# The order of VectorE's and ScalarE's work in the node stage of a graph network: statistics, scales and features ahead of the MLP's first addition

## The chip, the cores and the metric

One core of one Trainium2 chip. The metric is the device time of one execution in microseconds (us), lower is better, median of 3 runs. All data are float32.

## The reference

A graph of 12,500 nodes with 256 features and 200,000 edges with 96 features, sorted by destination. Two layers, each added to its input; cut to what matters:

```python
h = relu(layernorm(x))
# layer 0: an MLP on the node and what its incoming edges give
out1 = segment_sum(edge_attr, dst); cnt = segment_sum(1, dst)
out2 = where(cnt > 0, segment_max(edge_attr, dst), 0)
out3 = out1 / maximum(cnt, 1)
f = concatenate([h, out1, out2, out3, u[0]], axis=1)       # 256 + 3*96 + 64
x1 = x + (relu(f @ W1 + b1) @ W2 + b2) + h                 # W1: 608 x 1024, W2: 1024 x 256
# layer 1: two graph attention layers over the edges
h1 = relu(layernorm(x1))
g = gat(h1, W=g1, heads=4)                                 # first step of it: h1 @ g1
out = x1 + gat(elu(g), W=g2, heads=1)
```

## The kernel before

The kernel is a sequence of stages with a barrier of all engines behind each: `edge_chains` (sums and maxima of the edges' features, and already the part h @ W1 of the MLP, which goes to memory as `pre`), `node_mlp` (the node stage, the one that the change touches), `attention` and `close_first`, and again `attention` and `close_last`.

**The node stage** works on 49 tiles of 256 nodes. Every engine runs a function `step` for n = -1 to 49, the middle ones in a hardware loop, two steps per turn. Nothing but the order written in each engine's `step`, and semaphores between them, sets when what is done. In step n the stage has three tiles in hand:

- `nxt`, tile n+1: its input x is normalised (VectorE `statistics(nxt, 0)`, ScalarE `roots`, VectorE `inverse(nxt, 0)`, ScalarE `normal(nxt, 0)`, which writes h), and its edge features are scaled into `feat` (`features`, L1318 to L1322) for TensorE to transpose.
- `at`, tile n: the MLP. TensorE makes the first layer in four products of two chunks of 128 hidden columns each, 8 matmul records per product (L1138). VectorE adds `pre` to each product (`add_first(at, 0)` to `add_first(at, 3)`, L1332), ScalarE takes the Relu (`hidden`, L1206), TensorE makes the second layer (L1194).
- `prev`, tile n-1: VectorE adds the second layer to the residual (`result`, L1279; the result is x1), then its statistics (bn_stats L1261, bn_aggr L1265, variance L1267), ScalarE the root (L1210), VectorE `inverse(prev, 1)` (L1271, L1273), ScalarE the normalised rows h1 (L1215), TensorE transposes h1 (L1160), VectorE copies the transposed rows (L1367), and TensorE projects them with `wg` (L1185).

TensorE's order in a step: products 0 to 2 of `at`; the transposes of `prev`'s h1, ahead of which it waits for them; product 3; the transposes of `nxt`'s features (L1170, L1177); then twice a projection for `prev` (L1185) and a half of the second layer for `at` (L1194).

VectorE's order behind what the diff shows: the copy L1367 stands between `add_first(at, 2)` and `add_first(at, 3)`; then the copies of the transposed features, the two projections' outputs with `joined_edges` between them (L1302, L1308: edge rows for the tile after next), the rows x1 for memory (L1290), and `residual` (L1337, L1339), which reads h of `nxt`.

SP loads x and `pre` for the step after next and stores x1 and the projected rows. GpSimd, released by `joined_edges`, issues per step four gathers of single edges (L1095), two gathers of edge sums (L1102) and, from the tile with number 6 on, two scatters of scores to memory (L1110).

Of the kernel before, what the change touches and what calls it, by code (L numbers as in the profile page):

```python
# [954 lines left out]
def node_mlp(nc, s, io, dr, keep):  # L955
# [9 lines left out]
    KK = HC // 2  # L965
# [3 lines left out]
    with stage(nc, "node_mlp") as (c, sem):  # L969
# [74 lines left out]
        def all_steps(eng, step, first=-1):  # L1044
            steps(eng, first, LOOP, LOOP_END, NS + 1, step)
# [155 lines left out]
        @block.scalar  # L1201
        def _(a):
            def hidden(at, kk):
                a.wait_ge(m1_added, at.n * KK + (kk + 3))
                pair = hid[:, at.par, 2 * kk:2 * kk + 2, :]
                a.activation(pair, pair, ACT.Relu).then_inc(hid_ready, 1)  # L1206

            def roots(at, w):
                a.wait_ge(var_ready[w], at.n + 1)
                a.activation(root[:, w, :], var[:, w, :], ACT.Sqrt).then_inc(root_ready[w], 1)  # L1210

            def normal(at, w, src, dst, done):
                a.wait_ge(nb_ready[w], at.n + 1)
                for t in range(2):
                    a.activation(dst[:, t, :], src[:, t, :], ACT.Relu, bias=nb[:, w, t:t + 1],  # L1215
                                 scale=rstd[:, w, t:t + 1]).then_inc(done, 1)

            def step(at, n):
                nxt, prev = at.plus(1), at.plus(-1)
                mlp = n is None or 0 <= n < NS  # L1220
                if n is None or n >= 1:
                    roots(prev, 1)
                if mlp:
                    hidden(at, 0)
                if n is None or n + 1 < NS:
                    roots(nxt, 0)
                if n is None or n >= 1:
                    normal(prev, 1, x1[:, prev.par, :, :], h1[:, :, :], h1_ready)
                if mlp:
                    hidden(at, 1)  # L1230
                    hidden(at, 2)
                if n is None or n + 1 < NS:
                    normal(nxt, 0, x[:, nxt.par, :, :], hrow[:, nxt.par, :, :], h_ready)
                if mlp:
                    hidden(at, 3)

            a.dma_start(wg[:, :, 0:XF], io["g1_w"].rearrange("(k p) n -> p k n", p=P)).then_inc(wg_in, 16)
            for m, name in enumerate(("g1_src", "g1_dst")):
                a.dma_start(att[:, m, :], io[name].rearrange("h d -> (h d)").unsqueeze(0)
                            .to_broadcast([P, XF])).then_inc(wg_in, 16)  # L1240
            a.dma_start(g2b[:, :], io["g2_b"].unsqueeze(0).to_broadcast([P, XF])).then_inc(g2b_in, 16)
            a.dma_start(g1b[:, 0:XF], io["g1_b"].unsqueeze(0).to_broadcast([P, XF])).then_inc(g1b_in, 16)
            a.dma_start(wg2[:, :, 0:XF], io["g2_w"].rearrange("(k p) n -> p k n", p=P)).then_inc(late_in, 16)
            for m, name in enumerate(("g2_src", "g2_dst")):
                a.dma_start(att2[:, m, :], io[name].rearrange("h d -> (h d)").unsqueeze(0)
                            .to_broadcast([P, XF])).then_inc(late_in, 16)
            all_steps(a, step)

        @block.vector
        def _(v):  # L1250
# [25 lines left out]
            def result(at, n):  # L1276

                v.wait_ge(m2_ready, at.n + 1)
                v.tensor_tensor(x1[:, at.par, :, :], res[:, at.par, :, :],  # L1279
                                pM2[:, :].rearrange("p (t f) -> p t f", t=2), ALU.add).then_inc(x1_ready, 1)  # L1280
                v.wait_ge(x1_ready, at.n + 2)
                statistics(at, 1, x1[:, at.par, :, :])
# [44 lines left out]
            def add_first(at, kk):  # L1327

                if kk == 0:
                    v.wait_ge(pre_in[at.par], at.half * 16 + 16)  # L1330
                v.wait_ge(m1_ready, at.n * KK + (kk + 1))
                v.tensor_tensor(hid[:, at.par, 2 * kk:2 * kk + 2, :].rearrange("p k n -> p (k n)"), pM1[kk][:, :],  # L1332
                                pre[:, at.par, 2 * kk:2 * kk + 2, :].rearrange("p k n -> p (k n)"), ALU.add).then_inc(m1_added, 1)
# [8 lines left out]
            def step(at, n):  # L1342
                nxt, prev = at.plus(1), at.plus(-1)
                back = n is None or n >= 1
                front = n is None or n + 1 < NS
                mlp = n is None or 0 <= n < NS
                if back:
                    result(prev, None if n is None else n - 1)
                if mlp:
                    add_first(at, 0)  # L1350
                if front:
                    v.wait_ge(x_in[nxt.par], nxt.half * 16 + 16)
                    statistics(nxt, 0, x[:, nxt.par, :, :])
                if back:
                    inverse(prev, 1)
                if mlp:
                    add_first(at, 1)
                if front:
                    inverse(nxt, 0)
                    if n is not None and n <= 1:  # L1360
                        joined_edges(nxt, n + 1)
                    features(nxt)
                if mlp:
                    add_first(at, 2)
                if back:
                    v.wait_ge(gt_ready, prev.n + 1)
                    v.tensor_copy(h1T[:, :, :].rearrange("p i n -> p (i n)"), pG[:, :]).then_inc(gt_copied, 1)  # L1367
                if mlp:
                    add_first(at, 3)
                if front:  # L1370
                    v.wait_ge(t_ready, nxt.n + 1)
                    v.tensor_copy(fT[:, nxt.par, 0:2, :].rearrange("p i n -> p (i n)"), pF0[:, :])
                    v.wait_ge(rest_ready, nxt.n + 1)
                    v.tensor_copy(fT[:, nxt.par, 2, :], pF1[:, 0:N2]).then_inc(t_copied, 1)
                if back:
                    for t in range(2):
                        v.wait_ge(go_ready, prev.n * 2 + (t + 1))
                        if t == 0 and (n is None or n >= 3):
                            v.wait_ge(g_out[prev.par], prev.half * 16)
                        v.tensor_copy(keep["ald"][:, bass.ds(prev.n * 2 + t, 1), :].rearrange("p o h -> p (o h)"),  # L1380
                                      pGo[:, XF + H:WG]).then_inc(ald_ready, 1)
                        v.tensor_copy(keep["als"][:, bass.ds(prev.n * 2 + t, 1), :].rearrange("p o h -> p (o h)"),
                                      pGo[:, XF:XF + H])
                        if n is not None and t == 0 and prev.n == 0:
                            v.wait_ge(g1b_in, 16)
                            v.wait_ge(g1b_filled, 1)
                        v.tensor_tensor(grow[:, prev.par, t, :], pGo[:, 0:WG], g1b[:, :], ALU.add).then_inc(go_copied, 1)
                        if t == 0 and (n is None or n + 2 < NS):
                            joined_edges(at.plus(2), None if n is None else n + 2)
                if back:  # L1390
                    biased(prev, None if n is None else n - 1)
                if front:
                    if n == -1:
                        v.wait_ge(b2_in, 16)
                    residual(nxt)
                if n == 0:
                    v.wait_ge(wg_in, 16 * 3)
                    project_attention(v, chain, wg, att, tmp, H)
                    v.sem_inc(projected, 1)
                    v.memset(g1b[:, XF:WG], 0.0).then_inc(g1b_filled, 1)  # L1400
                    v.wait_ge(edges_in, 32)
                    v.tensor_scalar(keep["dst0"][:, :], dst0[:, :], s.NP - 1, None, ALU.min)
                if n == 16:
                    v.wait_ge(late_in, 16 * 3)
                    project_attention(v, chain, wg2, att2, tmp, 1)
                    v.sem_inc(wg2_ready, 1)
# [4 lines left out]
            v.sem_inc(go_copied, 1)  # L1411
            v.sem_inc(m1_added, 2)
            all_steps(v, step)


# [366 lines left out]
```

## Time and profile before

| | |
|---|---|
| median of 3 runs | 6822.59 us (6811.17 to 6826.57) |
| the profiled execution's own time | 6822.27 us |
| span of that execution | 6820.3 us |
| busy share of the span: TensorE, VectorE, ScalarE, GpSimd | 23%, 68%, 46%, 58% |
| node stage, first to last `result` (L1279) | 702.8 to 1793.9 us |

The profile is of one execution. An engine counts as busy while one of its instructions runs; waits and DMA issues don't count. In the rows further down, PE is TensorE, PEld its weight loads, DVE VectorE, ACT ScalarE, POOL GpSimd; L1279 is line 1279 of the kernel. PEclk is the share of TensorE's full clock of 2.4 GHz that was granted; its two levels are 1.0 and 0.5 (1.2 GHz). Matmul ends are modelled. The releaser of a wait is inferred from semaphore events; "remote" and "issue" mean that no instruction was found that ended it.

### The profile page before, as it was taken

The page shows a single profiled execution, that of the slowest core. Times are in us where ns is not written, and L with a number is a line of the kernel's source. Part 1 is how long each engine was busy: PE and PEld are TensorE (multiplying, and loading weights), DVE is VectorE, ACT ScalarE, POOL GpSimd, SP SyncE. Part 2 cuts the span into 40 slices and gives each one's busy share as a digit, 9 for nine tenths or more (in the row PEclk, how much of TensorE's full clock was granted, in tenths as well). Part 3 has the DMA queues.
Part 4 walks back from the last instruction along what each step waited for, and adds up shares of the span by engine and source line. Part 5 has one row for each costly group of instructions (what it writes and reads, how often), then busy time and mean ns, then how long its engine had stood idle before and what let it go on. Part 6 is the DMA issues. An engine that isn't in the chain of part 4 may idle for free. (4 is left out here: it accounts for less than half of the span.)

```text
span 6820.3 us, 34527 instructions
## 1 busy us (share of the span) xinstructions
PE 1577.0 (23%) x7221; PEld 1277.1 (19%) x7221; DVE 4656.6 (68%) x8059; ACT 3168.9 (46%) x2937; POOL 3988.8 (58%) x3935
## 2 busy tenths in 40 slices
PE   6675888888500000000000004500000000000000
PEld 4554676766400000000000003400000000000000
DVE  8997656656567777777776674466766766766665
ACT  7984222222145555555554552345555555555540
POOL 1330333333466666667666646577777777777756
PEclk9998999999755555555555557755555555555555
DMA  9998332332355555555555544456555555555548
GB/s 339 372 381 312 103 106 93 100 97 93 101 190 188 187 187 190 193 192 198 197 185 184 189 175 128 108 178 205 183 184 201 184 184 196 188 184 189 189 164 302
DMA packets 358516, 1281.83 MB, mean 188 GB/s; under 512 B 83184, under 2 KB 175408, under 8 KB 328272
## 3 DMA queue, kind: packets, MB, share of 16 engines
q1 hardware_dynamic: 167984, 756.10, 29.9%
q0 software_dynamic: 180320, 471.38, 24.0%
q10 hardware_dynamic: 10048, 52.70, 1.9%
q14 instruction: 127, 1.04, 0.0%
q8 instruction: 37, 0.61, 0.0%
HBM read 676.46 MB, written 603.41 MB: 188 GB/s over the span
## 5 line engine op out<-in xcount | busy, mean ns | idle before, releaser
L162 POOL DMA_INDIRECT rows<-table_d,k_src x3128 | 3123.2, 998 | 1256.3 <-issue 1142.5
L217 ACT ACTIVATE rows<-totals 128x1472 f32<-128x1472 f32 x544 | 2088.9, 3863 | 1408.9 <-DVE totals L308 1042.9
L308 DVE TENSOR_TENSOR_SCAN totals<-mask,turned 128x1536 f32<-128x1536 f32 x544 | 1806.4, 3341 | 71.1 <-DMA g1b<-in_g_b 60.7
L180 PE MATMUL pB<-diag,k_ones 128*128 128x512 f32 (+1 forms) x4 | 2.9, 822 | 4405.9 <-DVE diag L327 2222.0
L299 DVE TENSOR_TENSOR turned<-rows,pT 128x1472 f32<-128x1472 f32 x544 | 916.1, 1684 | 0.0
L180 PEld LDWEIGHTS pB<-diag,k_ones 128*128 128x128 f32 x4 | 1.0, 312 | 4406.6 <-DVE diag L327 2222.3
L1095 POOL DMA_INDIRECT lone_ea<-in_ea,k_gather x196 | 202.1, 1031 | 640.4 <-DVE mid_feat L1308 565.6
L265 DVE TENSOR_TENSOR z<-rows,ad 128x92 f32<-128x92 f32 (+1 forms) x136 | 29.0, 214 | 643.0 <-DMA rows<-table_d,k_src 596.0
L720 PE MATMUL pH<-hT_pre,w1h 128*128 128x256 f32 x1568 | 410.6, 419 | 135.6 <-ACT hT_pre L598 109.3
L1138 PE MATMUL pM<-fT,w1e 128*128 128x256 f32 x1568 | 405.0, 416 | 1.5 <-issue 1.5
L1194 PE MATMUL pM<-w,hid 128*128 128x256 f32 x1568 | 360.1, 383 | 1.8 <-issue 1.3
L720 PEld LDWEIGHTS pH<-hT_pre,w1h 128*128 128x128 f32 x1568 | 320.6, 211 | 210.5 <-ACT hT_pre L598 125.0
L209 ACT ACTIVATE pT<-zm 128x92 f32<-128x92 f32 (+1 forms) x136 | 29.5, 217 | 666.3 <-issue 410.9
L1138 PEld LDWEIGHTS pM<-fT,w1e 128*128 128x128 f32 x1568 | 317.6, 208 | 64.6 <-issue 18.9
L664 POOL DMA_INDIRECT dst_rows<-in_dst,full_i x98 | 149.6, 1527 | 306.9 <-DVE full_i L779 279.0
L1332 DVE TENSOR_TENSOR hid<-pM,pre_in 128x512 f32<-128x512 f32 x196 | 134.9, 689 | 258.8 <-PE pM L1138 211.5
L1194 PEld LDWEIGHTS pM<-w,hid 128*128 128x128 f32 x1568 | 296.9, 191 | 52.7 <-ACT hid L1206 10.0
L1210 ACT ACTIVATE root<-var 128x2 f32<-128x2 f32 x98 | 19.9, 203 | 582.6 <-DVE var L1267 323.6
L1206 ACT ACTIVATE hid<-hid 128x512 f32<-128x512 f32 x196 | 122.7, 626 | 338.2 <-DVE hid L1332 337.1
L1439 POOL DMA_INDIRECT acc_c<-sums_d,k_gather x196 | 211.0, 1077 | 76.0 <-issue 60.7
L910 DVE SCALAR_TENSOR_TENSOR run<-run,joins,duo 128x96 f32<-128x96 f32 x783 | 243.5, 311 | 2.4 <-DMA rows_d<-run 1.5
L910 DVE SCALAR_TENSOR_TENSOR run<-run,parts_off,duo 128x96 f32<-128x96 f32 x783 | 243.4, 311 | 0.0
(248 smaller groups left out, 3808.7 us busy)
## 6 DMA issues: line engine op xcount, KB each, us to landing
sums_d<-rows SPq DMA_DIRECT2D x68, 3036.0 KB
sums_d<-rows SPq DMA_DIRECT2D x68, 2967.0 KB
ea<-in_ea SPq DMA_DIRECT2D x98, 768.0 KB
rows_d<-run SPq DMA_DIRECT2D x97, 768.0 KB
pre_d<-pre ACTq DMA_DIRECT2D x49, 1024.0 KB
pre_in<-pre_d SPq DMA_DIRECT2D x49, 1024.0 KB
rows<-table_d,k_src POOLq DMA_INDIRECT x3128
hrow_c<-table_d SPq DMA_DIRECT2D x98, 256.0 KB
```

Of the source, the lines that this page charges most:

```text
L162: p.indirect_dma_start(out=rows[:, g.slot, k, :], out_offset=None, in_=table, in_offset=bass.IndirectOffsetOnAxis(ap=keep["src"][:, e:e + ...
L217: a.activation(rows[:, g.slot, :, q * PD:(q + 1) * PD], totals[:, q, :, 1:].rearrange("p d k -> p k d"), ACT.Copy).then_inc(rowed, 1)
L299: return link.mark(v.tensor_tensor(into[:, :, 1:].rearrange("p d k -> p k d"), rows[:, g.slot, :, q * PD:(q + 1) * PD], weights[:, :, h:h ...
L308: v.tensor_tensor_scan(totals[:, q, :, :].rearrange("p d k -> p (d k)"), mask[:, g.n % 2, :, :].rearrange("p d k -> p (d k)"), turned[q % ...
L664: g.indirect_dma_start(out=rows[:, b % 2, q, :], out_offset=None, in_=tiles_of("dst"), in_offset=bass.IndirectOffsetOnAxis(ap=full_i[:, b ...
L720: mm = pe.matmul(pH[k % 4][:, 0:N2], w1h[:, i, k * P:(k + 1) * P], hT[:, n % 2, i, :], start=(i == 0), stop=(i == 1))
L910: v.scalar_tensor_tensor(out=run[:, g % BUFS, k, m, :], in0=before, scalar=by[:, e:e + 1], in1=duo[:, g % 2, m, k, :], op0=op0, op1=op1).t ...
L1095: g.indirect_dma_start(out=lone_ea[:, n % 2, t, i, :], out_offset=None, in_=io["ea"], in_offset=bass.IndirectOffsetOnAxis(ap=keep["gather" ...
L1138: mm = pe.matmul(pM1[kk][:, h * N2:(h + 1) * N2], w1e[:, i, cols], fT[:, at.par, i, :], start=False, stop=(i == 1), skip_group_check=True)
L1194: mm = pe.matmul(pM2[:, t * XF:(t + 1) * XF], hid[:, at.par, k, t * P:(t + 1) * P], w2[:, k, :], start=(k == 0), stop=(k == HC - 1), skip_ ...
L1332: v.tensor_tensor(hid[:, at.par, 2 * kk:2 * kk + 2, :].rearrange("p k n -> p (k n)"), pM1[kk][:, :], pre[:, at.par, 2 * kk:2 * kk + 2, :]. ...
L1439: g.indirect_dma_start(out=self.acc[:, n // PER % 2, j % self.CH, :], out_offset=None, in_=self.rows, in_offset=bass.IndirectOffsetOnAxis( ...
```

## The change

Only the order of calls in two `step` functions of the node stage differs. On VectorE `add_first(at, 0)` and `add_first(at, 1)` go behind `features(nxt)`. On ScalarE all four `hidden` go behind `normal(prev, 1, ...)` and ahead of `normal(nxt, 0, ...)`.

```diff
@@ ScalarE, step @@
                 if n is None or n >= 1:
                     roots(prev, 1)
-                if mlp:
-                    hidden(at, 0)
                 if n is None or n + 1 < NS:
                     roots(nxt, 0)
                 if n is None or n >= 1:
                     normal(prev, 1, x1[:, prev.par, :, :], h1[:, :, :], h1_ready)
                 if mlp:
-                    hidden(at, 1)
-                    hidden(at, 2)
+                    for kk in range(KK):
+                        hidden(at, kk)
                 if n is None or n + 1 < NS:
                     normal(nxt, 0, x[:, nxt.par, :, :], hrow[:, nxt.par, :, :], h_ready)
-                if mlp:
-                    hidden(at, 3)
@@ VectorE, step @@
                 if back:
                     result(prev, None if n is None else n - 1)
-                if mlp:
-                    add_first(at, 0)
                 if front:
                     v.wait_ge(x_in[nxt.par], nxt.half * 16 + 16)
                     statistics(nxt, 0, x[:, nxt.par, :, :])
                 if back:
                     inverse(prev, 1)
-                if mlp:
-                    add_first(at, 1)
                 if front:
                     inverse(nxt, 0)
                     if n is not None and n <= 1:
                         joined_edges(nxt, n + 1)
                     features(nxt)
                 if mlp:
+                    add_first(at, 0)
+                    add_first(at, 1)
                     add_first(at, 2)
```

## Rows read from the trace of the kernel before

**Rows 1.** Timeline of VectorE: start us, us, instruction, idle before and its releaser.

```profile
745.97 0.69 DVE L1279 TENSOR_TENSOR x_rows<-res,pM 128x512 f32<-128x512 f32 x1 [0.96 <-issue]
...
1738.86 0.69 DVE L1279 TENSOR_TENSOR x_rows<-res,pM 128x512 f32<-128x512 f32 x1 [0.81 <-PE pM L1194]
...
1757.26 0.69 DVE L1279 TENSOR_TENSOR x_rows<-res,pM 128x512 f32<-128x512 f32 x1 [0.81 <-PE pM L1194]
```

**Rows 2.** Waits of 746 to 1739 us: total us, times, longest.

```profile
DVE hid L1332 <- PE pM L1138: 200.3, 75, 4.6
...
PE pG_ L1160 <- ACT h_rows L1215: 153.8, 43, 6.4
```

**Rows 3.** Timeline of one step, 1226.07 to 1248.04, engine by engine.

```profile
1226.07 0.69 DVE L1279 TENSOR_TENSOR x_rows<-res,pM 128x512 f32<-128x512 f32 x1 [0.82 <-PE pM L1194]
...
1232.64 0.69 DVE L1332 TENSOR_TENSOR hid<-pM,pre_in 128x512 f32<-128x512 f32 x1 [4.49 <-PE pM L1138]
1233.25 0.74 DVE L1261 BATCH_NORM_STATS2 bn_st<-x_rows 128x6 f32<-128x256 f32 x2
...
1235.79 0.32 DVE L1318 TENSOR_SCALAR feat<-mid_feat,has 128x192 f32<-128x192 f32 x1
...
1236.97 0.69 DVE L1332 TENSOR_TENSOR hid<-pM,pre_in 128x512 f32<-128x512 f32 x1
1237.57 0.68 DVE L1367 COPY h1T<-pG_ 128x512 f32<-128x512 f32 x1
1238.52 0.69 DVE L1332 TENSOR_TENSOR hid<-pM,pre_in 128x512 f32<-128x512 f32 x1 [0.27 <-PE pM L1138]
...
1248.04 0.69 DVE L1279 TENSOR_TENSOR x_rows<-res,pM 128x512 f32<-128x512 f32 x1 [0.81 <-PE pM L1194]
...
1234.89 1.09 ACT L1215 ACTIVATE h_rows<-x_rows,nb,rstd 128x256 f32<-128x256 f32 x2
...
1227.03 5.45 PE L1138 MATMUL pM<-fT,w1e 128*128 128x256 f32 x24
1236.13 0.63 PE L1160 MATMUL pG_<-k_ident,h_rows 128*128 128x128 f32 x4 [3.65 <-ACT h_rows L1215]
...
1239.93 3.72 PE L1194 MATMUL pM<-w,hid 128*128 128x256 f32 x16
...
1230.18 0.98 POOL L1110 DMA_INDIRECT first_d<-k_ald,k_first  x1 [0.30 <-issue]
```

**Rows 4.** Timeline of two other steps: GpSimd's last of four scatters, VectorE's additions.

```profile
1718.78 0.97 POOL L1110 DMA_INDIRECT first_d<-k_ald,k_first  x1 [0.31 <-issue]
...
1721.41 0.69 DVE L1332 TENSOR_TENSOR hid<-pM,pre_in 128x512 f32<-128x512 f32 x1 [7.22 <-remote]
...
1741.86 0.69 DVE L1332 TENSOR_TENSOR hid<-pM,pre_in 128x512 f32<-128x512 f32 x1 [0.92 <-PE pM L1138]
...
1747.74 0.69 DVE L1332 TENSOR_TENSOR hid<-pM,pre_in 128x512 f32<-128x512 f32 x1 [0.27 <-PE pM L1138]
```

**Rows 5.** Stretches: length, busy us of each engine, PEclk, DMA share, GB/s.

```profile
746.00:1739.00 993.00, 839.23 (x4218) 692.43 (x4222) 591.93 (x1944) 209.93 (x430) 345.31 (x344) 0.94 0.31 97
1212.60:1217.00 4.40, 4.35 (x17) 3.66 (x18) 2.90 (x9) 2.11 (x5) 0.00 (x0) 0.62 0.00 0
1757.00:1775.00 18.00, 17.85 (x98) 14.90 (x97) 11.64 (x37) 4.90 (x10) 1.94 (x2) 1.00 0.09 28
```

**Rows 6.** Line 1320 over the stage; timeline where VectorE runs beside GpSimd.

```profile
L1320 DVE TENSOR_SCALAR feat<-mid_feat,inv x98: 243/249/370, 670.8 to 1764.1; 128x64 f32<-128x64 f32 x98
...
711.12 0.94 POOL L1095 DMA_INDIRECT lone_ea<-in_ea,k_gather  x1 [11.97 <-DVE mid_feat L1308]
...
711.71 0.37 DVE L1320 TENSOR_SCALAR feat<-mid_feat,inv 128x64 f32<-128x64 f32 x1
...
1068.15 0.30 DVE L1267 TENSOR_SCALAR var<-bn_mv 128x2 f32<-128x2 f32 x1
...
1068.49 0.20 ACT L1210 ACTIVATE root<-var 128x2 f32<-128x2 f32 x1 [13.11 <-DVE var L1267]
```

## The prediction

> **What bounds the kernel now.** I began with the page's slices of time, which show where each engine is busy: TensorE's busy part is the edge and node stages, up to about a quarter of the span, and the rest belongs to GpSimd and VectorE. The change touches the node stage alone, and the stages meet at barriers, so what one step of it gains is gained for the kernel, times the number of steps.
>
> I take `result`'s addition (L1279) as the start of a step, t = 0. The timeline of that line [rows 1] has 43 steps between 745.97 and 1738.86: 992.9 us, 23.1 us each. The step behind them, from 1738.86 to 1757.26, takes 18.4 us with the same matmuls. So 4.7 us of each of the 43 are no work. The list of waits over that stretch says where [rows 2]: VectorE waits 200 us ahead of L1332, the addition of the MLP, and TensorE 154 us, 43 times, for h1, the normalised rows that ScalarE makes at L1215. That is 3.6 us a step.
>
> The timeline of one step shows how these hang together [rows 3]. TensorE does the products 0 to 2 from 1227.03 to 1232.48 (t+6.4) and then stands idle 3.65 us until h1 is there. VectorE has x1's variance ready 4.49 us before 1232.64, at 1228.15 (t+2.1). But its queue holds `add_first(0)` next, and that starts at 1232.64 (t+6.6). Only behind it stand the statistics of the next rows (from 1233.25) and `inverse(prev)`, whose scales let ScalarE's normalisation run from 1234.89 to 1235.98, and TensorE's transposes begin at 1236.13. h1 needs nothing of the MLP: it is late because its scales stand in VectorE's queue behind an addition that waits.
>
> Why does `add_first(0)` wait so long? It needs 8 of the 24 matmuls, done near t+3. In the step that starts at 1738.86, where GpSimd issues no scatter at that time, it does start at t+3.0 [rows 4]. In the usual step GpSimd issues two scatters of scores (L1110); the second ends at 1231.16 (t+5.1) [rows 3], and the addition starts 1.5 us behind it. In one step four are issued in a row; the last ends at 1719.75 and the addition starts at 1721.41, 1.7 us behind it [rows 4]. I conclude that TensorE's reports reach VectorE late while a scatter is under way. The profile doesn't show why; I call it the hold. The hold by itself is not what TensorE waits for: it does harm through the order of VectorE's queue.
>
> **The second cost, the clock.** Behind the idle time the granted clock can fall. In the step before the one of rows 3 it is 0.62 from 1212.60 to 1217.00 [rows 5], part of the time at 1.2 GHz. Over the 43 steps it is 0.94; over 1757 to 1775, where TensorE is busy 17.85 of 18.00 us, it is 1.00.
>
> **The change, part by part.** No instruction is added or removed, and no DMA.
>
> VectorE: ahead of `add_first(0)` now go the statistics of the next rows and `inverse(prev)` (1233.25 to 1234.89, 1.6 us), `inverse(next)` and the features (1235.79 to the third addition's start at 1236.97, 1.2 us) [rows 3]. Between 1234.89 and 1235.79 lie the second addition, 0.6 us, and `inverse(next)`, 0.3 us; I allow it 0.4, since it now follows its root directly. That is 3.2 us put into a hole of 4.5 us. From t+2.1: x1's scales at t+3.7, the next rows' at t+4.1, the features at t+5.3. The first addition can start at t+6.6 as before, so the hole covers it all. Were the hold gone, the additions would start at t+5.3 instead of t+3, and the fourth of them, the one that matters, would still be in time, as the next lines show.
>
> h1: ScalarE starts at t+3.75 and needs 1.09 us. It is ready at t+4.9, and TensorE comes to it at t+6.4: the idle 3.65 us goes whole, and with it the cause of the half clock.
>
> TensorE then does the four transposes, 0.5 us, and the fourth product, a third of the 5.45 us, to t+8.8.
>
> VectorE: three additions from t+6.6 at 0.6 us each (the copy L1367 follows the third one by 0.60 us, 1236.97 to 1237.57 [rows 3]), the copy at t+8.4, the fourth addition at t+9.05. In the step at 1738.86 it starts at 1747.74, t+8.9 [rows 4]. From the start of the fourth addition to the second layer's first matmul it is 1.41 us (1238.52 to 1239.93), from there to the next `result` 8.11 us (1248.04) [rows 3]. Together 18.57, and I take 18.6 us. The floor is the 18.4 us of rows 1.
>
> ScalarE: the Relus run 0.6 us each behind their additions; the normalisation of the next rows now comes behind the fourth, at about t+10.4 to 11.5. Its reader is `residual`. That stands in VectorE's queue behind the wait for the second projection, which TensorE makes when the first half of the second layer is through: 3.7 us (L1194 in rows 3) behind t+10.5, so not before t+14. Those 2.5 us and more cover the move; without them it would cost its 1.1 us.
>
> The other queues: `features(next)` waits for edges and `statistics(next)` for x of the next step. SP issues x for the step after next at a step's end and `joined_edges` works a step ahead, so nearly a whole step of 18 us lies between. GpSimd is released by `joined_edges`, at a fixed distance from the second layer, so its eight issues end 5.1 us into the next step as before, and the hold stays at t+6.6.
>
> One of the 43 is the step with four scatters, whose addition starts 2.7 us later than usual: 21.3 us there. What else is done once (`project_attention`, the first steps) I leave as it is.
>
> Sum: 43 x 18.6 + 2.7 = 802.5 us instead of 992.9: 190.4 us saved. The profiled execution's own time is 6822.27 us, 0.3 us from the median of the runs, 6822.59. Forecast: 6822.3 - 190.4 = 6632 us.
>
> **A price that the trace only bounds.** The features are tensor_scalar instructions from SBUF to SBUF, and at t+4.1 to 5.3 they now run beside the second scatter (t+4.1 to 5.1). In an early step they ran beside a gather of GpSimd [rows 6]: the gather took 0.94 us, no longer than the scatters of rows 3 and 4 without such company (0.98, 0.97), and the second L1320, 0.25 us by its median, took 0.37. So these rows price it at 0.12 us on VectorE per GpSimd issue, inside the hole: nothing. The upper end is that the second scatter waits for all the features and the hold ends 1.5 us later. I take the low end, since these are the same instructions.
>
> The Trainium skill, "SBUF — State Buffer", section "Who interferes with whom", speaks against the change here. It says that a VectorE tensor_scalar in a two-port mode and a GpSimd instruction exclude each other for their whole length, and that GpSimd's writing of descriptors is what is held up. By it the scatters and the hold would come later; the gather of 0.94 us does not bear out a full block.
>
> **The rivals.**
>
> A, the forecast: 18.4 to 18.9 us per step.
>
> B, the features push the second scatter: hold and additions 1.5 us later, a step of 20.1 us. 43 x 20.1 + 2.7 = 867.0, 126 us saved: 6696 us. For it: scatter and features now lie at the same time. Against it: rows 6. This is the case in which the rule of the page above would hold in full.
>
> C, the hold catches ScalarE's reports too. Then the next rows' root, done near t+3.7, reaches VectorE at t+6.6; `inverse(next)` and the features (1.6 us) end at t+8.2, and the additions start there: a step of 20.2 us, 6701 us. For it: no row shows a report of ScalarE arriving inside a hold. Against it: VectorE's report to ScalarE gets through. The root at 1068.49 starts 0.04 us behind the variance's end at 1068.45, which had a scatter beside it [rows 6].
>
> D, nothing comes of it: the hold follows what VectorE does and moves to t+11.1, where 11.1 + 2.45 (to the fourth addition) + 9.52 is again 23.1 us. Against it: the hold ends 1.5 to 1.7 us behind a scatter in both cases seen.
>
> E, the other side: without its rests TensorE isn't granted the full clock. A step has 0.99 x 18.4 = 18.2 us of matmuls at full speed; with a share f of the time at half it takes 18.2 / (1 - f/2), which passes 23.1 us at f = 0.42. All at half would be 36.4 us a step and 7397 us. Against it: 1.00 in the last row of rows 5 with TensorE 99% busy.
>
> **How the numbers follow.** A 0.72, B 0.10, C 0.09, a mixture that is still faster 0.03, D 0.02, E 0.04. The likeliest gives 6632 us; its own range is 18.2 to 18.9 us per step, 6615 to 6645. The range of 8 in 10 takes in a few us more from the first steps, and B and C at the other end: 6612 to 6705. A measurement of this kernel tells about 0.2%, 14 us, from no change: faster 0.94, same 0.02, slower 0.04.
>
> **What would show it.** Right: no wait of TensorE ahead of L1160; 18.6 us from `result` to `result`; statistics, scales and features between L1267 and the first L1332, with about 1 us idle behind them; a clock of 1.00 over the stage; the stages behind as long as before. B shows as scatters that are longer or further apart, C as a gap ahead of the next rows' reciprocal, E as half clock while TensorE is busy. The prediction is wrong if the first addition starts later than t+6.6, where each 0.1 us costs 4.3 us, or earlier and the step still isn't shorter than 18.6.

## The result, and the profile after

| | before | after |
|---|---|---|
| median of four runs each | 6824.58 us (6811.17 to 6874.94) | 6639.62 us (6621.58 to 6668.59) |
| the profiled execution's own time, its span | 6822.27, 6820.3 us | 6668.59, 6666.8 us |
| node stage, first to last `result` | 702.8 to 1793.9 us | 739.9 to 1633.4 us |

The change makes the kernel faster: the ratio of the runs is 0.9704, with a 95% interval of 0.9670 to 0.9739 (the quotient of the medians is 0.973). The forecast was 6632 us.

The two profiled executions differ by less than the node stage does, and the table shows why. The node stage fell from 1091.0 to 893.5 us, by 197.5. The edge stage ahead of it, whose code is the same, took 37 us longer in the execution profiled after. The profiles of all the kernels below fall into the same two groups there: the first `result` comes at 701 to 707 us or at 735 to 740 us, whatever the kernel. The profile before is of the short kind, the profile after of the long kind; two of the four runs after, 6621.58 and 6625.81 us, lie where 6822.27 less the 197.5 us would be. And 7 us more lie behind the node stage, 5 of them between the two attentions. So 197.5 - 37 - 7 = 153.5 us, the difference of the spans.

The timeline of `result` (L1275 after) answers to [rows 1]:

```profile
783.87 0.69 DVE L1275 TENSOR_TENSOR x_rows<-res,pM 128x512 f32<-128x512 f32 x1 [0.96 <-issue]
...
1578.98 0.69 DVE L1275 TENSOR_TENSOR x_rows<-res,pM 128x512 f32<-128x512 f32 x1 [0.81 <-PE pM L1194]
1597.11 0.69 DVE L1275 TENSOR_TENSOR x_rows<-res,pM 128x512 f32<-128x512 f32 x1 [0.81 <-PE pM L1194]
```

The 43 steps take 795.1 us, 18.49 each, where they took 23.09; without the one with four scatters it is 18.43. The step behind them takes 18.13, where it took 18.4. The waits over those 43 steps (total us, times, longest) answer to [rows 2], and the stretches below them (length, busy us of PE, PEld, DVE, ACT and POOL, PEclk, DMA share, GB/s) to [rows 5]:

```profile
ACT hid L1206 <- DVE hid L1328: 132.5, 86, 5.3
...
DVE hid L1328 <- PE pM L1138: 44.5, 37, 1.3
...
PE pG_ L1160 <- ACT h_rows L1215: 1.2, 1, 1.2
```

```profile
784.00:1579.00 795.00, 789.42 (x4218) 654.23 (x4217) 590.44 (x1944) 212.32 (x430) 351.62 (x344) 1.00 0.38 122
1225.50:1244.00 18.50, 18.39 (x102) 15.23 (x106) 13.91 (x46) 4.93 (x10) 8.14 (x8) 1.00 0.38 121
```

TensorE's wait for h1 is gone: 153.8 us in 43 waits before, one of 1.2 us now. TensorE is busy 789 of 795 us, at the full clock. The work is the same, 4218 matmul records and 1944 instructions of VectorE; only the rests are gone. VectorE still waits 44.5 us ahead of its additions, where it was 200.3.

One step from its `result` at 1225.48 (engine by engine; "x3" is three instructions of one line in a row) answers to [rows 3]:

```profile
1228.70 0.17 DVE L1263 TENSOR_SCALAR var<-bn_mv 128x2 f32<-128x2 f32 x1
...
1229.34 0.16 DVE L1269 SCALAR_TENSOR_TENSOR nb<-bn_mv,rstd 128x2 f32<-128x2 f32 x1
1229.58 0.32 DVE L1314 TENSOR_SCALAR feat<-mid_feat,has 128x192 f32<-128x192 f32 x1
...
1230.17 0.47 DVE L1314 TENSOR_SCALAR feat<-mid_feat,has 128x192 f32<-128x192 f32 x1
...
1232.06 1.89 DVE L1328 TENSOR_TENSOR hid<-pM,pre_in 128x512 f32<-128x512 f32 x3 [1.07 <-PE pM L1138]
...
1233.87 0.68 DVE L1361 COPY h1T<-pG_ 128x512 f32<-128x512 f32 x1
...
1234.46 0.68 DVE L1328 TENSOR_TENSOR hid<-pM,pre_in 128x512 f32<-128x512 f32 x1
...
1229.16 1.09 ACT L1215 ACTIVATE h_rows<-x_rows,nb,rstd 128x256 f32<-128x256 f32 x2
...
1231.73 0.60 PE L1160 MATMUL pG_<-k_ident,h_rows 128*128 128x128 f32 x4
...
1229.60 0.98 POOL L1110 DMA_INDIRECT first_d<-k_ald,k_first  x1 [0.30 <-issue]
```

The hole in VectorE's queue, 4.49 us before, is now filled with the statistics, the scales and the features; 1.07 us of it are left. h1 is ready at 1230.25, some 1.5 us ahead of TensorE, which comes to it without a wait. The first addition still starts at t+6.6 (1232.06), 1.5 us behind the end of the second scatter (1230.58): the hold, the late arrival of TensorE's reports at VectorE, is where it was. After the change it harms nothing but the fourth addition, which stands behind three others and a copy that all start with it.

The step with four scatters (`result` at 1557.74) answers to [rows 4]:

```profile
1564.42 0.97 POOL L1110 DMA_INDIRECT first_d<-k_ald,k_first  x1 [0.30 <-issue]
...
1567.08 1.29 DVE L1328 TENSOR_TENSOR hid<-pM,pre_in 128x512 f32<-128x512 f32 x2 [3.83 <-remote]
```

The last scatter ends at 1565.39 and the additions start 1.7 us behind it, at t+9.3, as before. The step takes 21.24 us.

### The profile page after: what moved, and what is told of

It is laid out like the page before. It is cut to its first block and busy times, and to the rows that moved or that the text cites. A ratio compares the mean times of both kernels' runs of the same rounds, so it can differ in the third digit from the quotient of the medians.

```text
span 6666.8 us, 34527 instructions
## 1 busy us (share of the span) xinstructions
PE 1584.1 (24%) x7221; PEld 1283.6 (19%) x7221; DVE 4655.7 (70%) x8059; ACT 3180.9 (48%) x2937; POOL 3990.8 (60%) x3935
## 5 line engine op out<-in xcount | busy, mean ns | idle before, releaser
L720 PE MATMUL pH<-hT_pre,w1h 128*128 128x256 f32 x1568 | 463.6, 460 | 120.9 <-ACT hT_pre L598 108.8
L720 PEld LDWEIGHTS pH<-hT_pre,w1h 128*128 128x128 f32 x1568 | 361.3, 237 | 208.5 <-ACT hT_pre L598 126.8
L1138 PE MATMUL pM<-fT,w1e 128*128 128x256 f32 x1568 | 364.6, 386 | 1.3 <-issue 1.3
L1138 PEld LDWEIGHTS pM<-fT,w1e 128*128 128x128 f32 x1568 | 293.4, 192 | 55.4 <-issue 18.7
L202 ACT ACTIVATE mask<-k_same 128x1472 f32<-128x1472 f32 x136 | 196.5, 1445 | 43.6 <-DVEq L250 32.7
L296 DVE TENSOR_SCALAR turned<-totals,fade 128x64 f32<-128x64 f32 x536 | 197.4, 368 | 28.3 <-DVE totals L308 18.7
```

Source lines behind the costliest of these rows:

```text
L202: a.activation(mask[:, g.n % 2, :, 1:], held, ACT.Copy).then_inc(masked, 1)
L296: link.mark(v.tensor_scalar(into[:, :, 0], totals[:, q, :, GROUP], fade[:, h:h + 1], None, ALU.mult))
L720: mm = pe.matmul(pH[k % 4][:, 0:N2], w1h[:, i, k * P:(k + 1) * P], hT[:, n % 2, i, :], start=(i == 0), stop=(i == 1))
L1138: mm = pe.matmul(pM1[kk][:, h * N2:(h + 1) * N2], w1e[:, i, cols], fT[:, at.par, i, :], start=False, stop=(i == 1), skip_group_check=True)
```

## The experiments

One thing has to be known ahead of all of them. They ran on three chips, with the kernel before beside them each time. There the kernel before takes 6147 to 6168 us (medians of 19 and more runs for each chip), not 6825, and the hold occurs in none of the profiles. The chip of the first result is not named on record; that it is another one is concluded from the times, and it is called the first chip below. Most of the expectations were written for the chip of the first result, and several miss for that reason alone. Single runs of one kernel scatter between two levels some 35 us apart, the two lengths of the edge stage, so that ratios have intervals of 0.25 to 0.45% either way. The lengths of the steps in the profile tell more.

**1. The scatters later, in the order before.**

```diff
                 if n >= BACK:
+                    g.wait_ge(ald_ready, 2 * n - 5)
                     scores_to_edges(n - BACK)
```

> The old order of VectorE and ScalarE; only GpSimd's two scatters of scores wait until the step's first projection has been read, so that they run at about t+11 to 13.5 of a step instead of t+2.8 to 5.1. Theory (the scatters hold TensorE's reports, and the old order passes that on to h1): the first addition starts at t+3.0 in all steps, TensorE's idle time ahead of L1160 is gone, a step is 18.4 us, and 43 x 4.7 = 202 us are saved: about 6620 us without touching the order. Rival (the wait belongs to the old order of VectorE itself, the scatters only lie beside it): steps stay at 23.1 us and the time at 6823.

Measured: 6141.61 us against 6155.47, ratio 0.9986 (0.9956 to 1.0016). 18.45 us per step. The first addition starts at t+3.0, and it does so in experiment 3 too, where the scatters are where they always were.

**2. Only the scales.** Statistics and `inverse(prev)` ahead of the first addition; `inverse(nxt)` and the features stay behind the second. ScalarE as after. The lines are against the kernel before, whose `add_first(at, 0)` ahead of the statistics goes.

```diff
                     inverse(prev, 1)
                 if mlp:
+                    add_first(at, 0)
                     add_first(at, 1)
                 if front:
                     inverse(nxt, 0)
```

> Half of the change: statistics of the next rows and x1's scales ahead of the first addition, but the next rows' scales and the features stay between the second and third addition, as before; ScalarE in the new order. Theory: h1 is in time as in the full change, but the 1.5 us of scales and features now lie between the additions from t+6.6 on, the fourth addition starts at t+10.5 and a step takes 20.0 us: 43 x 20.0 + 2.7 = 863, about 6692 us, 65 us over the full change. Rival (all of the gain is h1's scales): 18.5 us a step, as the full change, 6628 us.

Measured: 6116.94 us, ratio 0.9967 (0.9941 to 0.9994); 18.16 us per step.

**3. ScalarE's part alone.** The order of ScalarE is that of after, VectorE's that of before.

> ScalarE's part of the change alone, VectorE in the old order. Theory: h1 waits for x1's scales on VectorE at t+8.8, not for ScalarE, so nothing changes: 23.1 us a step, 6823 us within 10. Rival (a Relu ahead of h1 holds it up): up to 0.6 us a step less, 26 us, 6797 us.

Measured: 6131.33 us, ratio 0.9991 (0.9964 to 1.0018); 18.50 us per step. The timeline of one step:

```profile
1218.72 0.69 DVE L1275 TENSOR_TENSOR x_rows<-res,pM 128x512 f32<-128x512 f32 x1 [0.81 <-PE pM L1194]
...
1221.72 0.69 DVE L1328 TENSOR_TENSOR hid<-pM,pre_in 128x512 f32<-128x512 f32 x1 [0.92 <-PE pM L1138]
...
1224.05 1.09 ACT L1215 ACTIVATE h_rows<-x_rows,nb,rstd 128x256 f32<-128x256 f32 x2
1225.25 0.42 PEld L1160 LDWEIGHTS pG_<-k_ident,h_rows 128*128 128x128 f32 x4 [0.51 <-issue]
...
1222.84 0.98 POOL L1110 DMA_INDIRECT first_d<-k_ald,k_first  x1 [0.30 <-issue]
```

The second scatter ends at t+5.1, just as in [rows 3], and yet the first addition starts at t+3.0. So a scatter is not enough for the hold. On this chip h1 is only some 0.5 us late (the idle time of the weight loads, PEld, ahead of L1160). With VectorE in the order before, this run and those of 1 and 8 stand for the kernel before on such a chip: 18.45 to 18.50 us per step.

**4. TensorE kept busy.** Four matmuls more ahead of its wait for h1, into a bank that is written anew later; order before.

```diff
                         products(at, kk)
+                    for k in range(4):
+                        pe.matmul(pF0[:, 0:N2], w1e[:, 0, 0:P], fT[:, at.par, 0, :], start=True, stop=True,
+                                  skip_group_check=True)
```

> The kernel before, with four more matmuls of 128x256 (their result unused) on TensorE between the product 2 and its wait for h1: 1.7 us of work inside the 3.65 us of idle time. They change no wait. Theory (part of the loss is the half clock behind the idle time): the clock is 1.00 over the stage, the fourth product takes 1.9 us in all steps, and each step takes 21.9 to 22.0 us, the length that the steps at full clock have: 43 x 1.1 = 47 us saved, 6776 us. Rival (the clock costs nothing here, the longer fourth product is covered by VectorE): 6823 us.

Measured: 6227.08 us, ratio 1.0125 (1.0081 to 1.0169); 19.86 us per step. The filler takes 1.89 us, finds only 0.5 us of rest and costs 1.4 us per step; TensorE is busy 699.96 of the 700 us from 800 to 1500. It says that TensorE is the bound there, and nothing on the clock.

**5. The scatters later, in the order after.** The edit of 1 in the kernel after.

> The changed kernel with the scatters moved as in the run on the old order. Theory: no hold at t+3, the additions start at t+5.3 behind the features, the fourth at t+8.6 with the product; a step takes 18.13 us like the changed kernel's last three (18.13 each), 0.36 us less than its mean of 18.49: 43 x 0.36 = 15 us, and 3 more in the step with four scatters: about 6620 us. Rival: the hold moves onto another report of TensorE (the second projection at t+14.9, or the features' transposes), and a step takes 18.5 us or more.

Measured: 6150.52 us against 6168.49, ratio 0.9960 (0.9935 to 0.9985); 18.16 us per step, the first addition at t+5.2.

**6 and 7. More work ahead of the first addition.** The features are made once more (6) and three times more (7) into a tile that nobody reads; order after.

```diff
                 ins.then_inc(feat_ready, 1)
+                v.wait_ge(more_ready, at.n * 6)
+                for m in range(1):
+                    for t in range(2):
+                        whole = mid[:, 1, t, :, :]
+                        v.tensor_scalar(more[:, m, t, 0:2 * EF], whole.rearrange("p m f -> p (m f)"),
+                                        has[:, 0:1], None, ALU.mult).then_inc(more_ready, 1)
...
```

> The changed kernel with VectorE's six feature instructions done once more into an unused tile, ahead of the first addition: 1.2 us. Theory (the hole of the hold covers what stands in it until t+6.5): nothing or up to 0.1 us a step, 6640 us within 8. Rival (VectorE is the bound in the step): 1.2 us a step, 53 us more.

> The same with three more sets, 3.6 us. Theory: the hole has 1.1 us left, so 2.5 us a step stick out: the additions start at t+9.0 instead of t+6.55 and a step takes 20.9 to 21.0 us, 43 x 2.45 = 105 us more than the changed kernel, about 6745 us. Rival (VectorE the bound from the start): 3.6 us a step, 155 us more, 6795 us.

Measured: 6142.82 us, ratio 0.9982 (0.9957 to 1.0007), 18.31 us per step; and 6253.51 us, ratio 1.0170 (1.0128 to 1.0212), 20.90 us per step. One step of the second, from its `result` (L1277) on:

```profile
1210.11 0.69 DVE L1277 TENSOR_TENSOR x_rows<-res,pM 128x512 f32<-128x512 f32 x1 [0.81 <-PE pM L1196]
...
1219.07 1.88 DVE L1341 TENSOR_TENSOR hid<-pM,pre_in 128x512 f32<-128x512 f32 x3
1220.86 0.67 DVE L1374 COPY h1T<-pG_ 128x512 f32<-128x512 f32 x1
1221.46 0.68 DVE L1341 TENSOR_TENSOR hid<-pM,pre_in 128x512 f32<-128x512 f32 x1
```

The first set of 1.2 us is nearly free (0.15 us): the additions go from t+5.2 to t+6.4, and their last one from t+8.62 to t+8.76. Three sets, 3.5 us, push the last one to t+11.1, 2.5 us late, and the median step grows by the same 2.5 us, from 18.13 to 20.61. So about 1 us of cover was left, and what goes beyond it ahead of the first addition is paid in full. Experiment 6 also shows that the first addition at t+6.4 by itself costs little in this order. The mean of 7, 20.90 us, meets the 20.9 to 21.0 expected partly by chance: that was worked out for a chip with a hold, and 0.3 us of the mean come from a few longer steps, five of them (21.9 to 22.6 us) with a granted clock of 0.92.

**8. Gathers in the scatters' place.** Order before; GpSimd reads edge rows into a spare tile instead of writing the scores to memory, so the scores are left out.

```diff
-                        out=dr["first1"], out_offset=bass.IndirectOffsetOnAxis(ap=keep["first"][:, j:j + 1], axis=0),
-                        in_=keep["ald"][:, j, 0:H], in_offset=None).then_inc(keep["first_out"], 16)
+                        out=spare[:, j, :], out_offset=None, in_=io["ea"],
+                        in_offset=bass.IndirectOffsetOnAxis(ap=keep["gather"][:, 1, j:j + 1], axis=0),
+                    ).then_inc(keep["first_out"], 16)
...
```

> The kernel before with a gather of edge rows (128 rows of 96 elements, to an unused tile) in the place of each scatter of scores, with the same wait ahead of it. The scores are left out: memory keeps its zeros there, and what follows computes with them. Theory (only the scatter holds TensorE's reports, a gather does not): the first addition starts at t+3.0 and a step takes 18.4 us. Rival (any indirect DMA in the queue does): the first addition starts 1.5 us behind the last issue, near t+6.6, and a step takes 23.1 us.

Measured: 6147.86 us, ratio 0.9988 (0.9961 to 1.0015); 18.46 us per step. Without a hold to remove, it decides nothing between scatters and gathers. The trace of the kernel before on the first chip says more. It has gathers beside a report of TensorE in one step and none in another:

```profile
1244.18 0.96 POOL L1095 DMA_INDIRECT lone_ea<-in_ea,k_gather  x1 [0.30 <-issue]
...
1244.69 0.16 DVE L1380 COPY k_ald<-pGo 128x4 f32 x1 [2.06 <-PE pGo L1185]
...
1753.91 0.16 DVE L1380 COPY k_ald<-pGo 128x4 f32 x1 [2.06 <-PE pGo L1185]
```

The copy waits the same 2.06 us for the projection in both, and so does `result` for the second layer, 0.81 us, with a gather running up to 1248.04, the moment at which it starts. So these gathers hold nothing there.

**9. The kernel after, on such a chip.**

> The changed kernel itself, beside the kernel before on the chip of this job. If this chip shows the hold: 18.5 us a step against 23.1, ratio 0.970. If it shows none, as the chips of the other experiments: the additions start at t+5.2 behind the features, the fourth with the product at t+8.6, and a step takes 18.15 us instead of 18.45: 43 x 0.3 = 13 us, ratio 0.998. Rival: the change costs something where there is no hold, since the first three additions start 2.2 us later than in the old order: ratio 1.00 or above.

Measured: 6156.20 us against 6146.72, ratio 0.9994 (0.9967 to 1.0021). The same two kernels that are 3% apart on the first chip are not to be told apart here. The attentions are faster too, as a line of the page's fifth part shows (busy us, mean ns of one, idle before):

```profile
L162 POOL DMA_INDIRECT rows<-table_d,k_src x3128 | 2974.1, 951 | 952.8 <-issue 952.8
```

The same line on the first chip, kernel after:

```profile
L162 POOL DMA_INDIRECT rows<-table_d,k_src x3128 | 3123.9, 999 | 1257.8 <-issue 1147.7
```

The gathers of the attentions take 951 instead of 999 ns, and GpSimd's idle time ahead of them is 305 us less: 455 of the 515 us by which the two spans differ. A step takes 18.16 us, the first addition is at t+5.2. From 18.50 (experiment 3) to 18.16 the change is still worth 14 us over 43 steps. Behind the node stage this execution took 12 us longer than that of 3, 9 of them between the attentions, a part that varied from 355 to 371 us over the experiments.

**10, 11 and 12. A hold made by hand.** TensorE reports the products 0, 1 and 2 together at the end of product 2; nothing else changes. 10 is the order before, 11 the order after, 12 the order of experiment 2.

```diff
-                mm.then_inc(m1_ready, 1)
+                if kk == 2:
+                    mm.then_inc(m1_ready, 3)
+                elif kk == 3:
+                    mm.then_inc(m1_ready, 1)
```

> The kernel before, with TensorE reporting its products 0 to 2 together at the end of product 2 (one increment of 3) instead of each by itself: a hold made by hand, to t+6.4, on any chip. Theory: it is the late reports and VectorE's order alone that made the 23.1 us steps: additions from t+6.45, h1 at t+9.9, idle time of 3.5 us ahead of L1160, half clock in some of the steps behind it, 22 us where the clock stays full and 23.4 where it falls, 43 x 4.6 = 198 us more than the kernel before on a chip without hold. Rival (something else of the first chip made the steps long): 18.5 to 19 us a step.

> The changed kernel with the same hold made by hand. Theory: the work moved ahead fills the hole, the step takes 18.4 to 18.5 us with a clock of 1.00, about 12 us more than the changed kernel without a hold. Rival: 19 us or more.

> Only statistics and x1's scales moved ahead (the next rows' scales and the features between the second and third addition), with the hold made by hand. Theory: additions at t+6.45 and t+7.05, the third at t+9.2, the fourth at t+10.4, 19.9 us a step: the features' place in the hole is worth 1.45 us of the 4.6. Rival (only h1's scales matter): 18.5 us a step.

| | median, us | ratio to before, 95% | us per step | additions, from t |
|---|---|---|---|---|
| 10, order before | 6395.11 | 1.0401 (1.0364 to 1.0438) | 23.15 | 6.45, 8.61, 10.78, 13.84 |
| before, first chip | 6824.58 | | 23.09 | 6.47, 8.61, 10.81, 13.63 |
| 11, order after | 6168.37 | 1.0009 (0.9985 to 1.0034) | 18.41 | 6.45, 7.06, 7.66, 8.86 |
| after, first chip | 6639.62 | | 18.49 | 6.51, 7.12, 7.72, 8.91 |
| 12, scales only | 6225.76 | 1.0134 (1.0090 to 1.0179) | 19.92 | 6.45, 7.06, 9.23, 10.43 |

The hold by hand brings both steps of the first chip back, to a few hundredths of a microsecond in nearly every addition (medians over the steps of the timeline). Waits from 800 to 1500 us of 10 and two of its steps as stretches:

```profile
DVE hid L1335 <- PE pM L1138: 172.7, 60, 4.5
...
PE pG_ L1163 <- ACT h_rows L1218: 106.7, 30, 3.7
```

```profile
1202.97:1224.81 21.84, 18.32 (x102) 15.15 (x102) 13.73 (x45) 4.80 (x10) 8.10 (x9) 1.00 0.32 103
1224.81:1248.34 23.53, 20.01 (x102) 16.39 (x103) 13.73 (x46) 4.89 (x10) 8.10 (x9) 0.93 0.30 95
```

TensorE waits 3.6 us for h1 in each of 30 steps, as in [rows 2]. Behind that rest the granted clock stays full in the first of the two steps and falls in the second (0.93 over the step, so part of it at 1.2 GHz), and TensorE needs 20.01 instead of 18.32 us for the same 102 matmul records. That splits the loss of 4.65 us per step (23.15 - 18.50): a step at full clock takes 21.84, so 3.3 are the later h1, and the other 1.3 are, on average, mostly the clock.

The waits of 12, same stretch:

```profile
DVE hid L1331 <- PE pM L1138: 97.9, 35, 3.0
...
PE pF L1173 <- DVE feat L1321: 29.6, 34, 0.9
```

With only the scales ahead, TensorE finds h1 ready. But the next rows' scales and the features now stand between the held additions: TensorE waits 0.9 us a step for the features, and the fourth addition comes at t+10.43 instead of 8.86. That is 1.5 us per step more than 11. So under a hold the scales give 3.2 of the 4.7 us and the place of the features the rest; without one, experiment 2 is as good as the whole change (18.16 both).

## Why the prediction was right

**The bound.** h1 late through the order of VectorE's queue: shown. The change takes the wait away on the first chip, and experiment 10 makes it, with its size and the fall of the clock, out of a kernel that doesn't have it, by nothing but later reports of the products.

**The terms.** The forecast was 18.6 us per step without the extra of the four scatters, measured 18.43 (18.49 with it, where the sum had 18.66); the first addition at t+6.6, measured 6.3 to 6.6; the fourth at t+9.05, measured 8.91, right behind the copy as foreseen; the step with four scatters 21.3, measured 21.24. The saving of the 43 steps is 197.8 us for 190.4. The edge stage's two lengths, 37 us apart, were no term of the sum, so that part of how near 6632 and 6639.62 lie is luck. The clock is 1.00, and h1 is there before TensorE. ScalarE's moved normalisation costs next to nothing (experiment 3 against 1: 18.50 and 18.45, both without a hold).

**A term that was left out.** I took 18.4 us as the floor, from a step without scatters. That step still held a wait of its own, the 0.5 us of experiment 3, since the scales of its h1 too stood behind the first addition. The order after goes down to 18.13 there, in the last three steps and in nearly every step of experiment 9.

**The rivals.** B, the features push the second scatter: refuted. The scatters' issues in the step above are apart as before, and their median over the stage is 1.00 us, where it was 0.99 (the longest 1.08 instead of 1.00). The features do meet them: both L1314 above run beside the second scatter, the first took 0.32 us as elsewhere, the other 0.47. The prediction bounded this from below at 0.12 us per issue; it is 0.15, inside the hole. The Trainium skill, "SBUF — State Buffer", section "Who interferes with whom", has such a pair exclude each other for an instruction's whole length. The trace agrees that they interfere, but 0.15 us is far less than the 0.98 us for which the scatter runs; whether the instruction was in the page's two-port mode no run here shows.

C, a hold of ScalarE's reports: refuted, the next rows' reciprocals and the features ran on at once, and VectorE idles only ahead of the addition. D, the hold moves with VectorE: refuted, t+6.6 as before. E, no full clock for a busy TensorE: refuted by 1.00 over 795 us.

**What the forecast did not see.** Its size rests on the hold, and the hold belongs to the chip, or to the occasion, of the first result. The prediction tied it to the scatters. On the first chip the tie holds in both kernels, with one exception: t+3.0 without a scatter (t+5.1 or 5.2 behind the features in the order after), t+6.3 to 6.7 with two, t+9.3 with four. The addition comes 1.2 to 1.7 us behind the end of the last scatter's issue. The exception is the step before at 998.23, with two scatters at their usual place and the first addition at t+4.85, ahead of the second one's end. But the same scatters at the same place do nothing on the chips of the experiments, so they are at most half of the cause.

That it is the reports that come late, and not the other thing that the first addition waits for, the load of `pre`, can be read from the semaphore updates kept with the trace. In the step of [rows 3] TensorE's first product ends at 1229.03, the second at 1230.76 and the third at 1232.48, and their three updates stand at 1232.62, 1232.71 and 1232.80, one behind the other; in experiment 3 each stands 0.01 or 0.02 us behind its product. The load of `pre` for this step was issued two steps ahead, at 1193.89, and such a load takes 4.9 us in the experiments. In the exception the first update came at t+4.76, between the two scatters' transfers, and the second was held again, to t+6.23. Nor are the transfers slower: the last packet of the second scatter ends at t+5.86 in that step and at t+5.87 in the same step of experiment 3, and the updates on the first chip follow the last packet by 0.3 to 0.9 us. One difference in the record goes with it: the two traces of the first chip hold 28,454 and 27,632 semaphore updates, those of the experiments 89,207 to 90,312. Some two thirds are missing there, so a releaser that they name is less certain; whether that has to do with the hold is not shown.

Experiments 1, 5 and 8 were meant to separate it and could not, and 10 to 12 imitate what the hold does, not what makes it. What it is stays open. Where there is none, the change is worth 0.3 us per step, some 0.2% of the run, about as little as a comparison of whole runs can tell: 0.9994 in experiment 9, and 0.9967 and 0.9960 in 2 and 5, which have the same 18.16 us per step.

## What to carry to other kernels

Look for what stands in a queue behind a wait without needing what is waited for: here x1's scales behind an addition that needed TensorE. Put such work ahead of the wait as long as it fits the hole, and count what else is in the same place (the features, 1.5 us per step). A price that hangs on a delay whose cause the trace doesn't show may not exist on the next chip; the order after has the merit that it is hardly touched either way (18.41 with the hold, 18.16 without), where the order before varies from 18.5 to 23.15.

## What the hardware showed that was not expected

The same program takes 6825 us in the first result and 6147 to 6168 us on the three chips of the experiments, with the same instructions. Most of the difference, some 450 us, lies in the attentions: indirect DMA issues of 999 against 951 ns and more idle time between them. Some 200 us are the hold, during which VectorE sees TensorE's first product 3.5 us late (first addition at t+6.5 instead of t+3.0; 6.3 us late with four scatters). Finished products are then reported all at once, 0.09 us apart, while ScalarE's and VectorE's own reports pass without such a delay (`inverse(prev)` and `inverse(nxt)` ran inside the hold in the order after). Another 45 us lie between the attentions.
